# An experts stage that opens with its first unit: weight split beside the attention, last group's norm and routing among the units

## The reference, cut to what matters

```python
x = x + _L0_xattn_ref(ctx_2048, _layernorm(x, axis=-1), mask, mask, W_src, b_src, W_tgt, b_tgt, W_out, b_out)
x = x + _L0_ffn_ref(_layernorm(x, axis=-1), Wg, Wu, Wd, Wr, temperature)
```

```python
inh = sigmoid(x @ Wr / temperature)
in_zone = (inh >= GOLDEN_LOWER) & (inh <= GOLDEN_UPPER)
dist = abs(inh - GOLDEN_CENTER)
w = exp(-dist / 0.1) * in_zone        # unless no expert is in the zone:
fb = exp(-dist / 0.3)                 # then the two largest of fb, normalized
```

## Time and profile before

| what | us |
|---|---|
| median of three executions | 2359.65 (2358.11 to 2359.82) |
| the profiled execution, its own time | 2357.55 |
| its span in the profile | 2355.7 |
| TensorE busy, share of the span | 1996.4, 85% |
| VectorE busy, share | 1475.8, 63% |
| ScalarE busy, share | 1093.0, 46% |
| GpSimd busy, share | 750.8, 32% |
| granted TensorE clock over the span | 0.936 of full |

### The profile page before, as it was taken

The page is one execution under the profiler, slowest core; times in us unless marked ns, Lnnn a source line. Parts: engine busy times, 40 slices in busy tenths (PEclk is TensorE's granted clock), DMA queues, the critical chain, the costliest instruction groups (busy, mean ns, idle before and its releaser), DMA issues.

```text
span 2355.7 us, 35006 instructions
## 1 busy us (share of the span) xinstructions
PE 1996.4 (85%) x12078; PEld 1367.8 (58%) x12078; DVE 1475.8 (63%) x4614; ACT 1093.0 (46%) x2670; POOL 750.8 (32%) x752
## 2 busy tenths in 40 slices
PE   4888888988799998788799998579787798998679
PEld 3554556766455564455557787467454466666546
DVE  7666546444565557788734874798686755667663
ACT  2333344544433332577612565687574225666232
POOL 3221133112122232235551553554433331111353
PEclk9999999999799999999989999789798899999889
DMA  6999602000100002101161456000230000000100
GB/s 240 330 329 339 224 1 86 20 18 1 59 1 1 1 1 88 37 22 44 57 252 57 138 155 214 13 1 1 94 111 32 1 1 17 1 2 1 39 1 36
DMA packets 40302, 180.38 MB, mean 77 GB/s; under 512 B 6816, under 2 KB 24352, under 8 KB 36992
## 3 DMA queue, kind: packets, MB, share of 16 engines
q1 hardware_dynamic: 32496, 157.04, 19.8%
q0 software_dynamic: 7632, 21.11, 2.6%
HBM read 154.93 MB, written 98.89 MB: 108 GB/s over the span
## 4 chain that ended last, share of the span: by engine, by line
PE 62%; DVE 18%; ACT 11%; POOL 4%; issue 4%; DMA 1%; DVEq 0%; POOLq 0%; SPq 0%; ACTq 0%
PE ps L216 39%; PE ps L739 5%; ACT BIG L816 4%; PE ps L711 3%; PE ps L1953 3%; PE ps L758 3%; PE ps L281 2%; ACT BIG L291 1%; PE ps L1965 1%; DVE XN L272 1%; DVE BIG L291 1%; PE ps L845 1%; DVE BIG L779 1%; PE ps L1357 1%; DVE SML L257 1%
## 5 line engine op out<-in xcount | busy, mean ns | idle before, releaser
L216 PE MATMUL ps<-BIG 128*128 128x256 f16 (+2 forms) x1616 | 340.0, 360 | 26.3 <-DVE BIG L2554 12.9
L816 ACT ACTIVATE BIG<-BIG,SML 128x256 f32<-128x256 f32 (+1 forms) x768 | 302.6, 482 | 20.2 <-DVE SML L779 20.1
L216 PEld LDWEIGHTS ps<-BIG 128*128 128x128 f16 (+1 forms) x1616 | 223.6, 140 | 120.1 <-issue 64.5
L739 PE MATMUL ps<-CST,BIG 128*128 128x128 f32 x1408 | 219.2, 291 | 51.4 <-ACT BIG L816 33.3
L739 PEld LDWEIGHTS ps<-CST,BIG 128*128 128x128 f32 x1408 | 161.8, 147 | 128.8 <-ACT BIG L816 84.3
L636 POOL TENSOR_TENSOR BIG<-BIG 128x512 f16<-128x512 f32 x120 | 142.3, 1187 | 293.3 <-ACT BIG L570 265.1
L216 PE MATMUL ps<-XN,BIG 128*128 128x512 f16 x864 | 205.5, 394 | 14.2 <-ACT BIG L547 5.3
L779 DVE CUSTOM_DVE_ANT_0 BIG<-ps,BIG 128x256 f32<-128x256 f32 x512 | 181.3, 420 | 26.8 <-PE ps L711 26.5
L291 ACT ACTIVATE BIG<-ps 128x512 f32<-128x512 f32 (+1 forms) x240 | 127.0, 563 | 147.1 <-PE ps L739 113.0
L220 POOL TENSOR_SCALAR SML<-SML 128x4 f32<-128x4 f32 (+1 forms) x88 | 25.0, 285 | 504.4 <-DVE SML L260 246.3
L291 DVE COPY BIG<-ps 128x512 f32<-128x512 f32 (+1 forms) x176 | 110.3, 638 | 91.3 <-PE ps L739 81.8
(11 more groups left out here) (405 smaller groups left out, 3938.7 us busy)
## 6 DMA issues: line engine op xcount, KB each, us to landing
slots<-in_zeros SPq DMA_DIRECT2D x28, 2640.0 KB, 66.8
WA<-slots SPq DMA_DIRECT2D x95, 132.0 KB, 2.3
BIG<-in_l1e SPq DMA_DIRECT2D x2, 4224.0 KB, 20.0
BIG<-spread SPq DMA_DIRECT2D x16, 512.0 KB, 5.5
BIG<-in_l0e SPq DMA_DIRECT2D x8, 768.0 KB, 7.9
BIG<-in_ctxT SPq DMA_DIRECT2D x8, 512.0 KB, 7.2
BIG<-in_ctxT SPq DMA_DIRECT2D x16, 256.0 KB, 3.1
BIG<-in_ctx SPq DMA_DIRECT2D x16, 256.0 KB, 3.4
```

Source lines behind the costliest of these rows:

```text
L216: m = T.e.matmul(ps, l, r, start=i == 0, stop=i == len(pairs) - 1)
L739: m = T.e.transpose(PS[r][:, o:o + P], c["SM"][n % 2 * 4 + i][:, q, tok(k)], ident)
L816: A.e.activation(s[:, q, 0:kn[q]], s[:, q, 0:kn[q]], ACT.Exp, bias=mx[:, q:q + 1], scale=-1.0).then_inc(*(A.sig("exp", p, n, i) if q else ...
```

## The change

1. The buffers PT of phase 1 leave WA0. Three lie in RING at 10752 to 12287 (the place of expert 7, not loaded yet), five in free parts of SCR. WA0's two slots are thereby free in phase 1.
2. `first_split_2` is given to the attention as `extra`: the split of experts 0 and 1, with high and low parts written in pieces of 512 columns (six each); on TensorE one step later.
3. The prologue of phase 2 is gone. VectorE still does statistics and scaling of group 3 ahead of the first unit (GpSimd its root); its turn, copies, f16 pair and logits and then the routing are steps between the half units. VectorE's routing goes one step at a time for two steps and then two steps at a time (`once`, `twice`).
4. In phase 1 GpSimd takes the roots of groups 0 to 2 at even b from 4 on, and VectorE does the scaling, two moves after the statistics.

The diff, cut to its core:

```diff
@@ -890,14 +890,6 @@
                 G.wait_ge(*G.last())
                 G.e.memset(v[:, :, :, c["dh"]], 1.0).then_inc(*G.sig("ones", c["p"], i))
-        def spare_wa0():
...
         def spare_ring():
             o = [8192]
@@ -907,8 +899,9 @@
             return get
         def shared_1():
-            c = attend(1, 8, [range(0, 4), range(4, 8)], [2 * P, 2 * P], scratch((0, 3072), (5632, 6656)), spare_wa0(),
-                       "AAAA", scratch((3328, 5376)))
+            own, spare = scratch((6656, 7680), (12800, 13824), (14848, SCRN)), [RING[:, o:o + 512] for o in range(10752, 12288, 512)]
+            c = attend(1, 8, [range(0, 4), range(4, 8)], [2 * P, 2 * P], scratch((0, 3072), (5632, 6656)),
+                       lambda n: spare.pop() if spare else own(n), "AAAA", scratch((3328, 5376)))
             get = scratch((11776, 12800), (13824, 14848))
             c["KB"], c["QB"] = ([get(512).rearrange("p (k s) -> p k s", k=2) for _ in range(2)] for _ in range(2))
             c["mrow"], c["mcol"] = SCR[:, 7680:9728], sml[:, 200:216]
@@ -1085,8 +1078,11 @@
                 V.e.bn_aggr(mv[:, i, :], st6[:, i, :]).then_inc(*(V.sig("mean", p, g) if i % 4 == 3 else V.step()))
             if g == NG - 1:
                 norm_scale(V, p, g)
+            elif p == 2:
+                yield from pause(2)
+                norm_scale(V, p, g)
             if turn_of[p]:
-                yield from pause(6 if p == 2 else 7)
+                yield from pause(4 if p == 2 else 7)
                 if p == 2 and g:
                     logits_dve(2, g - 1)
                 norm_copy(V, p, g, 1)
@@ -1147,7 +1143,7 @@
             if ends_later(p, g):
                 return
             norm_root(p, g)
-            if g < NG - 1:
+            if g < NG - 1 and p != 2:
                 norm_scale(G, p, g)
         def add_bias(p, bias, gs):
@@ -1168,14 +1164,16 @@
             attend_pe(c, lambda b, h, q: c["QB"][b % 2][32 * (h % 4):32 * (h % 4) + 32, h // 4, tok(q)],
                       lambda b, h: [(n + "pc", b, m) for n in "qk" for m in range(2)] if h is None else
                       c["KB"][b % 2][32 * (h % 4):32 * (h % 4) + 32, h // 4, :],
-                      lambda b: [("vm", b)], lambda b: prep_1_pe(c, b), lambda b: post_out_pe(c, b, pairs(b)))
+                      lambda b: [("vm", b)], lambda b: prep_1_pe(c, b), lambda b: post_out_pe(c, b, pairs(b)),
+                      first_split_2("pe", c["RT"]) if 2 in phases else None)
         def l0_xattn_dve(c):
             attend_dve(c, lambda b, q: c["AM"][b % 2], 1.0 / math.sqrt(32.0), lambda b: prep_1_dve(c, b),
-                       lambda b: post_out_dve(c, b, True))
+                       lambda b: post_out_dve(c, b, True), first_split_2("dve") if 2 in phases else None)
         def l0_xattn_act(c):
-            attend_act(c, lambda b: iter(()), lambda b: post_out_act(c, b, True))
+            attend_act(c, lambda b: iter(()), lambda b: post_out_act(c, b, True),
+                       first_split_2("act") if 2 in phases else None)
         def l0_xattn_pool(c):
             if begun(1):
@@ -1190,8 +1188,8 @@
                     norm_root(1, NG - 1)
                 if b == 3:
                     add_bias(1, W[1]["bo"], [NG - 1])
-                if b >= 5 and b % 2 and after(1) is not None:
-                    spread_pool(after(1), (b - 5) // 2)
+                if b >= 4 and b % 2 == 0 and after(1) is not None and (b - 4) // 2 < NG:
+                    spread_pool(after(1), (b - 4) // 2)
         def load_1(c):
             if begun(1):
@@ -1556,6 +1554,35 @@
             for g in gens:
                 yield from g
+        def batch_split(c, x, engine, ring=None, size=4608):
+            if engine == "pe":
+                return split_pe(ring, x["key"], x["r"], 2 * c["per"])
+            if engine == "dve":
+                return split_dve(x["key"], x["parts"], x["r"], c["per"], x["loaded"], x["regs_free"], size=size)
+            return split_act(x["key"], x["parts"], x["r"], 2 * c["per"], x["free"], size=size)
+        def first_split_2(engine, ring=None):
+            gen = batch_split(F2["x"], F2["x"]["batches"][0], engine, ring, 512)
+            return chain(pause(1), gen) if engine == "pe" else gen
+        def splits(c, engine, ring=None):
+            own = [batch_split(c, x, engine, ring) for x in c["batches"]]
+            if phases[0] != c["p"]:
+                own[0] = iter(())
+            return own
+        def once(gen, n):
+            for _ in range(n):
+                next(gen, None)
+                yield
+        def twice(gen):
+            for _ in gen:
+                next(gen, None)
+                yield
         def needing(c, engine, gens):
             return [dict(it, need={engine: [gens[i // c["per"]]]}) for i, it in enumerate(c["items"])]
@@ -1563,9 +1590,9 @@
         def experts_pe(c, ring, first=None):
             p = c["p"]
             RG, RU, RD = ring
-            gens = [split_pe(RD, x["key"], x["r"], 2 * c["per"]) for x in c["batches"]]
+            gens = splits(c, "pe", RD)
             if ends_later(p, NG - 1):
-                finish(in_turn(chain(tail_pe(RD, p, NG - 1, 5), pause(4), logits_of(logits_pe, RD, p, NG - 1)), gens[0]))
+                first = chain(tail_pe(RD, p, NG - 1, 1), pause(2), logits_of(logits_pe, RD, p, NG - 1))
             tail, live = closing(c["order"], lambda g: [tail_pe(RD, after(p), g, 2)] if not ends_later(after(p), g) else [])
             units_pe(p, needing(c, "pe", gens), c["nh"], c["order"], c["lag"], RG, RU, RD,
                      in_turn(*([first] if first else []), chain(*gens, *([split_3("pe", RD)] if after(p) == 3 else []))), tail)
@@ -1573,9 +1600,12 @@
         def experts_dve(c, SB, HS, first=None):
             p = c["p"]
-            gens = [split_dve(x["key"], x["parts"], x["r"], c["per"], x["loaded"], x["regs_free"]) for x in c["batches"]]
+            gens = splits(c, "dve")
             if ends_later(p, NG - 1):
-                finish(in_turn(chain(tail_dve(p, NG - 1), pause(2), logits_of(logits_dve, p, NG - 1)), gens[0]))
+                late = tail_dve(p, NG - 1)
+                for _ in range(2):
+                    next(late)
+                first = chain(late, logits_of(logits_dve, p, NG - 1), pause(1), once(first, 2), twice(first))
             tail, live = closing(c["order"], lambda g: [tail_dve(after(p), g, ("acc", ("expert", p, c["n"] - 1), g, 1))]
                                  if not ends_later(after(p), g) else [])
             units_dve(p, needing(c, "dve", gens), c["nh"], c["order"], c["lag"], SB, HS,
@@ -1584,9 +1614,9 @@
         def experts_act(c, SB, HS, first=None):
             p = c["p"]
-            gens = [split_act(x["key"], x["parts"], x["r"], 2 * c["per"], x["free"]) for x in c["batches"]]
+            gens = splits(c, "act")
             if ends_later(p, NG - 1):
-                finish(tail_act(p, NG - 1))
+                first = chain(pause(1), tail_act(p, NG - 1), pause(2), first)
             tail, live = closing(c["order"], lambda g: [later(2, tail_act(after(p), g))] if not ends_later(after(p), g) else [])
             units_act(p, needing(c, "act", gens), c["nh"], c["order"], c["lag"], SB, HS,
                       in_turn(*([first] if first else []), chain(*gens, *([split_3("act")] if after(p) == 3 else []))), tail)
```

More of the change, by code:

```diff
@@ L891, in ones_columns @@
                 G.e.memset(v[:, :, :, c["dh"]], 1.0).then_inc(*G.sig("ones", c["p"], i))
-        def spare_wa0():
-            o = [512]
-            def get(cols):
-                o[0] += cols
-                return WA[0][:, o[0] - cols:o[0]]
-            return get
         def spare_ring():
```

## The result

| | before | changed |
|---|---|---|
| median of the comparison, four executions each, us | 2359.74 | 2340.01 |
| lowest and highest, us | 2358.11, 2360.36 | 2337.49, 2342.37 |
| ratio, 95% interval | | 0.991, 0.9896 to 0.9924 |
| the profiled execution, us (span) | 2357.55 (2355.7) | 2342.37 (2340.5) |

The kernel became faster by 19.7 us; the forecast was 2332.8, a gain of 26.9 against this median. It gained 7.2 us less than forecast. The time lies inside the range of 2324 to 2344, but not in the band that was called likeliest (A, 2326 to 2338).

What follows compares the result with a forecast made beforehand. TensorE was taken to bound the attention, with holes from waits for GpSimd's scaling and at the stage boundary. Terms -13.9 + 3.0 - 14.9 = -25.8 from 2357.55 gave 2331.8, stated as 2332.8 us, range 2324 to 2344.

Steps and rivals of the forecast that it cites:

- A: Whole kernel: the sum of the three parts holds, 2326 to 2338 us; chance 0.63.
- Part 1: Phase 1 attention: scaling of groups 0 to 2 on VectorE, GpSimd's root one batch earlier; -13.9 us.
- Part 2: Phase 1 attention: split of the first two experts beside it costs +3.0 us, between +1 and +7.
- The 1.2 at L1114: Attention, pair 15: two pieces of the split stand ahead of ScalarE's L1114, for which TensorE already waits; +1.2 us.
- The 1.2 at L882: Attention, pair 16: two pieces stand ahead of L873 and L882, on which TensorE's next transposes hang; +1.2 us.
- Part 3: Start of the expert stage: the first unit starts at once, without the prologue; gain 14.9 us.
- Everything after the expert stage shifts whole: Later stages: they move by the full gain, since their loads are issued by the stages' own events.
- Rival B: Attention gives nothing net, as TensorE waits for VectorE and ScalarE instead of GpSimd; 2340 to 2345 us, chance 0.14.
- C: Expert start: VectorE's queue slips and units 3 to 5 wait 5 us more; 2337 to 2340 us, chance 0.11.
- D: Attention: larger gain, the bank wait of 1.27 goes and pieces lie in slack; 2322 to 2326 us, chance 0.06.
- E: Attention's end: split unfinished, remaining pieces ahead of the first unit, +4 to +8; 2336 to 2340 us, chance 0.03.
- F: Units 0 to 5: TensorE waits for VectorE each half unit, clock at half level; slower, 2363.5 us, chance 0.03.

Runs made afterwards that it cites:

- the scaling alone: The kernel before with only the scaling of groups 0 to 2 on VectorE and GpSimd's roots at even b; median 2352.73 us, ratio 0.9965.
- the third profile: The changed kernel run a third time without edit, beside the kernels with earlier pieces; median 2341.63 us, ratio 0.9918.
- the two with earlier pieces: The changed kernel with the side work of phase 1's attention beginning at pair 3 or 2 instead of 6; medians 2337.99 and 2338.48 us.
- the first profile: The changed kernel in its first comparison with the kernel before; profiled execution 2342.37 us, median 2340.01 us.
- without the scaling: The changed kernel with the scaling of groups 0 to 2 back on GpSimd and its root at odd b; median 2358.43 us, ratio 0.9984.
- the two with the shift: The changed kernel with one or two VectorE reductions added at the end of phase 3, on another chip; medians 2373.50 and 2373.12 us, ratios 0.9908 and 0.9904.
- the one with the transposes: The changed kernel with four constant transposes ahead of each pair's first wait for exp in phase 4, on another chip; median 2361.99 us, ratio 0.9871.
- the second profile: The changed kernel run again without edit; median 2342.14 us, ratio 0.9911.

## Why the prediction was right, and where not

**Part 1, -13.9.** Right: 14.4 with the scaling alone. The two shares, from the distances between the pairs: from pair 9 to pair 13 it gains 9.0 (59.4 - 50.4), where 8.7 was said, and from pair 13 on, with group 1, 5.4 (65.04 - 59.67), where 5.2 was said. VectorE scaled as placed, at 484.38 behind L1014, at no cost to TensorE. The scaling took 1.38 in the attention, as at the boundary before: nothing held it. So the blocking of VectorE by GpSimd that the Trainium skill states (SBUF — State Buffer, "Who interferes with whom") did not come about at these places, since GpSimd's root ends before the scaling begins. That the concern was a real one for this operation the trace of the kernel before shows at another place, where GpSimd adds 1024 columns (L3765, 2.35 us) while VectorE scales: four scalings of the same size took 3.40 instead of 1.38.

```profile
337.88 2.35 POOL L3765 TENSOR_TENSOR X<-X,BIG 128x1024 f32<-128x1024 f32 x1
337.95 3.40 DVE L272 TENSOR_SCALAR XN<-X,SML 128x256 f32<-128x256 f32 x4 [1.41 <-POOL SML L222]
```

**Part 2, +3.0.** The mechanism (pieces in queues in order, on which TensorE's next transposes hang) was right; the size was too small and the places half right. The part measured 4.0 to 4.2 where the clock held (the third profile, and the two with earlier pieces) and 6.8 to 7.0 where it fell (the first profile, 176.6 - 169.8; without the scaling, 191.15 - 184.15). The third profile beside that of the scaling alone shows the terms. The reductions and the first handshake, put at 0, cost 0.2 up to pair 9 and 0.1 up to pair 13: right. The small operations of pair 13 and TensorE's small matmuls, 0.3 + 0.3, came to 0.9, 0.54 of it a new wait of L739 behind L1014. The 1.2 at L1114 in pair 15 did not come: that wait is 1.29 in the third profile, as it is before and with the scaling alone. In its place the 1.27 of L845 ahead of pair 14, which part 1 let stand, grew by 0.6. The 1.2 at L882 was 2.1. Where the clock fell too, the products behind the two waits ran at the half level for another 1.6 and 1.4, and the waits had been priced at their own length only.

**Part 3, -14.9.** Right: 71.63 - 56.66 = 15.0, and 13.3 where the first unit met a low clock. The new stalls were 0.27 and 0.85 = 1.1, in units 4 and 5, where 1.2 was laid out for units 3 to 5. The sum is partly luck, since the shares are exchanged: 0.9 was said for the table loads, which left 0.27, and 0.3 for the top-2 steps, behind which 0.85 stands. By the 2.66 a switch that the Trainium skill gives (ScalarE: Activation LUTs, "What ACT_TABLE_LOAD costs"), an estimate is that ScalarE's silu would have come 2.8 later there. The trace doesn't have it: the loads of the routing take 1.28 each in the changed kernel too, and the instruction behind each starts within 0.02 us of its end (load at 628.05, silu at 629.35).

**What the sum lacked.** "Everything after the expert stage shifts whole" failed, and it is the larger error: phase 4 took back 6.7, and the start up to 1.5. Up to the end of the experts the sum, 25.8, compares with the gain from pair 4 on. Six profiles have the changed kernel's code up to there (the three, the two with the shift and the one with the transposes), and their gains are 24.2, 23.3, 27.1, 27.1, 24.2 and 27.1 (472.24 less 448.02, 448.93, 445.18, 445.19, 448.02 and 445.19). With the clock up, the three parts give 14.4 - 4.0 + 15.0 = 25.4. Another 1.7 that no part of the sum holds comes at unit 8, which took 17.4 in all profiles of the kernel before and in the second of the changed one, and 15.7 in the other five, behind the same wait of 2.16 us where I read it (the first profile of each and the second of the changed kernel); why is open. Where the clock fell at the two waits of the attention, 2.8 are missing (24.2 against 27.1). In the second profile 3.8 are: 0.4 at the end of the attention and 1.7 each at the first unit and at unit 8.

With the 6.7 of phase 4 the forecast would have been 2339.5, against 2340.0 measured. That this is so close is luck in part, because the smaller errors (part 2, unit 8, the start) have both signs. Two of the signs that were named failed in the first profile: windows of the attention stood below 0.9 (552:564 and 576:588 at 0.86, 588:600 at 0.72; the last kind was there before, 0.78 at 600:612), and the first expert product came at 603.66, not within 3 of 598 (599.31 and 601.71 in the other two). The new waits behind L882 were 1.9, under the 3 that would have spoken against the mechanism.

Rival B's band, 2340 to 2345, holds the measured median at its edge, but for a wrong reason: the attention did give its gain. C, D and E did not happen: the start gave all that was said, the wait of 1.27 stayed or grew, and the last piece of the split ended at 582.48, some 20 us ahead of the end of the attention. F, a clock at half in units 0 to 5, did not happen; the largest wait there was 0.85.

## What to carry to other kernels

A sum over the stages that a change touches can be right to a few microseconds and the total still be off by more, when a later stage runs TensorE with many waits; here such a stage was granted a clock of 0.93 or 0.90 on the same instructions with the same idle time. Compare marks of the same instruction stage by stage, and look at more than one profile of each kernel, before a part is credited or blamed for the total: the scaling alone showed 7.7 us in the whole and 14.4 in its stage. In a loop whose engines hand work round, a piece put into an idle engine's queue is paid for where the next handed-over item stands behind it, even when TensorE's windows read 12.00 of 12 (1.13 us at L882 in pair 12).

## What the runs showed of the hardware that was not expected

The granted clock turned fixed sequences of instructions into stretches with two or three sharp values: 35.5 or 37.0 us for the start, 23.9 or 25.5 for pairs 13 to 15, 15.7 or 17.4 for unit 8, 209.4 or 216.0 to 216.7 for phase 4. In the same kernel the same wait, 1.87 and 1.88 us, was followed by the half level in one execution (L711 1.59, L739 1.97) and by the full one in another (1.15 and 1.09). And the chip of the runs with the shifts and the transposes took 35 us longer for the kernel before than the one of the other experiments (2395.27 against 2360.2 to 2360.4), while in its profile with the extra transposes the end of the experts came at 896.8, within 0.5 of the 896.4 and 896.6 of the others; what is longer there lies in later stages.
